# A fill of 1024 columns, with a wait, behind each of 80 indirect DMAs on GpSimd

## The reference, cut to what matters

```python
router_probs = softmax(einsum('bnc,ec->bne', x, router_w))
expert_weights, expert_idx = top_k(router_probs, 2)
expert_weights = expert_weights / (expert_weights.sum(axis=-1, keepdims=True) + 1e-09)
h = gelu(einsum('bnc,efc->bnef', x, expert_w1) + expert_b1)
out_all = einsum('bnef,ecf->bnec', h, expert_w2) + expert_b2
out_k = take_along_axis(out_all, expert_idx[..., None], axis=2)
return (out_k * expert_weights[..., None]).sum(axis=2)
...
x = x + gb * that      # gb: the layer's gate per channel
```

## Time and profile before

| | us |
|---|---|
| median of 3 runs | 1585.96 (1582.42 to 1589.9) |
| span of the profiled execution | 1571.4 |
| median minus that span | 14.6 |
| TensorE busy | 1254.3 (80%) |
| VectorE busy | 938.7 (60%) |
| ScalarE busy | 942.5 (60%) |
| GpSimd busy | 417.8 (27%) |

### The profile page before, as it was taken

How to read it: one execution, slowest core, us unless ns; L and a number is a source line. 1 busy time by engine, 2 the same in 40 slices (tenths; PEclk the granted TensorE clock), 3 DMA queues, 4 the chain that set the end, 5 groups by cost and what they waited for, 6 DMA issues and landing times. The chain is left out here.

```text
span 1571.4 us, 26317 instructions
## 1 busy us (share of the span) xinstructions
PE 1254.3 (80%) x8185; PEld 785.6 (50%) x8186; DVE 938.7 (60%) x2462; ACT 942.5 (60%) x1383; POOL 417.8 (27%) x460
## 2 busy tenths in 40 slices
PE   6996556695878658999999999999999796665660
PEld 4875556695875422333333333333333674564560
DVE  5563343473657747777777777877777575420222
ACT  4563512232325548999999899988999484332330
POOL 5254773414427720000000000000000004545333
PEclk9998768898988879999999999999999898777885
DMA  9600012222223653222222212222220411102222
GB/s 273 202 1 28 28 58 62 67 67 61 69 57 116 201 131 46 37 37 38 35 37 39 38 26 37 37 36 37 38 38 4 135 31 46 51 31 76 72 58 72
DMA packets 114776, 100.34 MB, mean 64 GB/s; under 512 B 10882, under 2 KB 99424, under 8 KB 114656
## 3 DMA queue, kind: packets, MB, share of 16 engines
q1 hardware_dynamic: 101256, 78.64, 20.9%
q0 software_dynamic: 8192, 16.79, 3.7%
q10 hardware_dynamic: 5208, 3.43, 0.9%
HBM read 54.51 MB, written 44.30 MB: 63 GB/s over the span
## 5 line engine op out<-in xcount | busy, mean ns | idle before, releaser
L2392 ACT ACTIVATE probs<-scores_ps 128x1024 f32<-128x1024 f32 x512 | 505.3, 1026 | 61.1 <-PE scores_ps L2419 56.5
L2419 PE MATMUL scores_ps<-q_pack,k_pack 64*128 64x512 f32 x1024 | 247.0, 494 | 47.1 <-ACT probs L2392 27.4
L2436 PE MATMUL pv_ps<-probs,v_pad 128*32 128x512 f32 x2048 | 275.0, 610 | 0.0
L2419 PEld LDWEIGHTS scores_ps<-q_pack,k_pack 64*128 64x128 f32 x1024 | 96.4, 185 | 321.9 <-ACT probs L2392 171.9
L1379 ACT ACTIVATE hidden_experts<-pre_experts 128x512 f32<-128x512 f32 x94 | 59.3, 631 | 184.8 <-DVE pre_experts L1313 79.9
L1401 PE MATMUL up_ps_experts<-x_t_experts,up_weights_now_experts 128*128 128x128 f32 x752 | 114.1, 300 | 68.8 <-issue 30.3
L1401 PEld LDWEIGHTS up_ps_experts<-x_t_experts,up_weights_now_experts 128*128 128x128 f32 x752 | 100.9, 209 | 75.2 <-issue 48.3
L2619 DVE TENSOR_SCALAR_CACHE_REDUCE junk<-sparse_scores,at 128x1024 f32<-128x1024 f32 x96 | 122.8, 1279 | 3.4
L2312 POOL COPY v_pad<-v 128x256 f32<-128x256 f32 (+1 forms) x16 | 6.3, 402 | 434.9 <-PE pv_ps L2436 434.8
L1408 PE MATMUL down_ps_experts<-weights_t,hidden_experts 128*128 x736 | 102.6, 285 | 0.0
L1313 DVE TENSOR_TENSOR pre_experts<-up_ps_experts,weights_t 128x512 f32<-128x512 f32 x94 | 64.5, 686 | 61.0 <-PE up_ps_experts L1401 31.2
(11 more groups left out here) (399 smaller groups left out, 2346.6 us busy)
## 6 DMA issues: line engine op xcount, KB each, us to landing
q_pack<-q_pieces_dram SPq DMA_DIRECT2D x120, 64.0 KB
k_pack<-k_pieces_dram SPq DMA_DIRECT2D x120, 64.0 KB
expert_rows_dram<-zeros SPq DMA_DIRECT2D x1, 6400.0 KB, 21.9
x_rows_experts<-expert_rows_dram SPq DMA_DIRECT2D x25, 256.0 KB
expert_rows_dram<-y_rows_experts SPq DMA_DIRECT2D x46, 128.0 KB
q_pieces_dram<-q_pieces_prep SPq DMA_DIRECT2D x8, 512.0 KB, 3.6
k_pieces_dram<-k_pieces_prep SPq DMA_DIRECT2D x8, 512.0 KB, 3.6
expert_rows_dram<-zeros SPq DMA_DIRECT2D x1, 2560.0 KB, 17.4
```

The costliest lines, as they stand in the source:

```text
L2392: act.activation(probs[:, kt % 2, 2 * pair : 2 * pair + 2, c * 512 : c * 512 + 512], scores_ps[n % 2][:].rearrange("p (h t) -> p h t", h=2 ...
L2419: ins = pe.matmul(scores_ps[n % 2][:, head * 512 : head * 512 + 512], k_pack[group % 2][rows, pair, kt * P : kt * P + P].bitcast(F32R), q_ ...
L2436: ins = pe.matmul(pv_ps[32 * j : 32 * j + 32, c, :], v_pad[:, group % 2, kt, j, :], probs[:, kt % 2, j, c * 512 : c * 512 + 512], start=(k ...
```

## The change

GpSimd gets a buffer `between` of 128 partitions x 1024 columns that nothing reads. A function `apart` fills it with zeros and settles, so that GpSimd's next instruction waits for the fill. `send_rows` and `gather` call `apart` after each indirect DMA, but only where it is given: in the expert loop, that is for the sends of batches 2 and 3 and the gathers of batches 0, 1 and 2. These are 5 chains of 16 DMAs, 80 fills. The stage in front and the stage behind the loop issue theirs as before.

```diff
--- before.py
+++ after.py
@@ -145,7 +145,7 @@
         step.settle()
         step(pool.tensor_tensor(h, h, bc(self.mod0[:, b, MOD0_PARTS.index(SB), :], NT), ALU.add))
 
-    def send_rows(self, g, pool, b, part=0, parts=1):
+    def send_rows(self, g, pool, b, part=0, parts=1, apart=None):
 
         rows = [(k, n) for k in range(2) for n in range(NT)]
         each = len(rows) // parts
@@ -153,6 +153,8 @@
             pool.indirect_dma_start(
                 self.rows, bass.IndirectOffsetOnAxis(ap=g.pick0[:, b, k, n : n + 1], axis=0), self.h[:, b * NT + n, :], None
             ).then_inc(g.rows_sent[b], 16)
+            if apart is not None:
+                apart()
 
     def loads(self, dram):
         return [
@@ -1184,12 +1186,14 @@
         a.clear_sems()
 
 
-def gather(pool, g, picked, b, parts, sem):
+def gather(pool, g, picked, b, parts, sem, apart=None):
 
     for k, n in parts:
         pool.indirect_dma_start(
             picked[k][:, b * NT + n, :], None, g.expert_rows0, bass.IndirectOffsetOnAxis(ap=g.pick0[:, b, k, n : n + 1], axis=0)
         ).then_inc(sem, 16)
+        if apart is not None:
+            apart()
 
 
 def experts0(nc, g, moe, picked):
@@ -1210,6 +1214,7 @@
         pre = a.sb("pre", [P, 2, FC, P])
         hidden = a.sb("hidden", [P, 2, FC, P])
         y_rows = a.sb("y_rows", [P, UNROLL, C])
+        between = a.sb("between", [P, 1024])
         xt_ps = a.ps("xt_ps", [C, UNROLL, P])
         up_ps = [a.ps(f"up_ps{i}", [P, FC, P]) for i in range(2)]
         down_ps = [a.ps(f"down_ps{i}", [P, 512]) for i in range(2)]
@@ -1278,17 +1283,22 @@
             @block.gpsimd
             def _(pool):
                 step = Steps(pool, sum_vec)
+
+                def apart():
+                    step(pool.memset(between[:], 0.0))
+                    step.settle()
+
                 for b in range(B):
                     if b >= SENT_EARLY:
                         moe.scale_and_shift(pool, step, b)
                         step.settle()
-                        moe.send_rows(g, pool, b)
+                        moe.send_rows(g, pool, b, apart=apart)
                     pool.wait_ge(g.rows_sent[b], 16 * 2 * NT)
                     pool.sem_inc(rows_here, moe.tiles)
                 pool.sem_inc(rows_here, max(moe.tiles, 2 * UNROLL))
                 for b in range(B - 1):
                     pool.wait_ge(y_free, b * (2 * AHEAD) + (2 * AHEAD + 1))
-                    gather(pool, g, picked, b, [(k, n) for k in range(2) for n in range(NT)], g.rows_picked)
+                    gather(pool, g, picked, b, [(k, n) for k in range(2) for n in range(NT)], g.rows_picked, apart=apart)
                     if 1 <= b <= EARLY:
                         pool.wait_ge(var_ready, b)
                         g.ln1.invert(pool, b - 1).then_inc(rstd_ready, 1)
```

## The result

| | us |
|---|---|
| changed kernel, median of 4 runs | 1520.68 (1519.96 to 1522.63) |
| kernel before, median of 4 runs | 1587.93 (1582.42 to 1592.06) |
| ratio, 95% interval | 0.9594 (0.9562 to 0.9625) |
| predicted | 1531, range 1515 to 1600 |

The changed kernel is 4.1% faster where the prediction's profile was taken. Both are measured, and the second half of this text is about what differs.

A forecast was written before the change was run, and what follows sets the result against it. TensorE, held up in five chains of back-to-back indirect DMAs, was taken as the bound. Loop end 474.3 to 419 gives 55 us: 1571.4 - 55 = 1516.4, plus 14.6 from span to median, 1531; range 1515 to 1600.

The forecast's parts named there:

- What bounds: Expert loop: TensorE's completions are held up while GpSimd issues indirect DMAs back to back, about 15 us in each of five chains.
- Price of the fill and period: In the five chains: a 1024-column fill takes 0.95 us, and DMA, fill and wait repeat every 2.19 us, at most 2.49.
- TensorE freed: In the chains: pauses free TensorE, with up to 3 us of lateness left per chain; chance 0.70.
- VectorE's wait at step 13: Loop step 13, where VectorE needs GpSimd's weighted sum of batch 0: a new wait of some 15 us, up to 18.
- at the steady pace 309.7: When step 13's transposes come, 14 steps of 7.71 us after the first at 201.78.
- the port's price: VectorE copies beside fills: 0.25 us a tile, some 18 tiles in each of two chains behind step 13; 4 us taken.
- The prediction's own sign: Stated check: if VectorE does not wait at step 13 for GpSimd's weighted sum, TensorE was not freed.
- The loop's end: Last copy of the expert loop: at 413, or 419 with lateness left in two chains, against 474.3 before.
- nothing behind the loop changes: Everything after the expert loop was taken to run as before, so the loop's 55 us gain carries through.
- From span to median: Whole kernel: median put 14.6 us above the profiled span, so 1516.4 became 1531.
- Its own 0.95 us each, pause or not: Rival, in chains: each DMA costs TensorE 0.95 us regardless, fills add port cost; 1586 to 1608, likeliest 1592; chance 0.10.
- Held as long as the chain lasts: Rival, in chains: TensorE stays held throughout the longer chain, losing 26.4 instead of 15 us each; 1643; chance 0.20.

The follow-up runs named there:

- experiment 11: Changed kernel without fills in the last chain, the gather of batch 2, which goes back to back; held: 1535.29 us against 1585.51, ratio 0.9694.
- experiment 12: Changed kernel with chains treated separately: landing waits, back to back, 32 columns, 512 columns, 1024 columns without the wait; held: 1542.24 us against 1585.51.
- free runs: Runs in groups where the unchanged kernel before takes 1373 to 1376 us (median) and its back-to-back chains keep TensorE busy.
- held ones: Runs in groups where the kernel before takes about 1586 us and TensorE loses time in back-to-back chains of indirect DMAs.
- kernel 6: The changed kernel run once more, unchanged, where nothing is held: 1398.73 us, ratio 1.0175 to the kernel before.
- kernel 5: The kernel before run once more, unchanged, with a profile, where nothing is held: 1377.07 us.
- experiments 4: Changed kernel with no fills; GpSimd instead waits after each of the 80 indirect DMAs until it has landed; free: 1441.85 us, ratio 1.0480.
- experiment 10: Kernel of experiment 12 plus a landing wait after each of the 64 sends in layer 1's experts; free: 1464.57 us against 1373.46.
- 2: Changed kernel with fills only behind the 48 gathers, the sends back to back; free: 1381.05 us against 1373.44, ratio 1.0053.

## Why the prediction was right, and where its steps were off

*What bounds.* Right for the place where it was measured. That TensorE loses its time beside indirect DMAs that follow each other closely is shown by experiments 11 and 12, chain by chain. The traces agree over the whole program: in the profile of before all 35 rows whose releaser is "remote" start inside a chain of indirect DMAs or at most 3.5 us behind its end, none in the 787 us between 512.8 and 1299.5, which have no such DMA. In the changed kernel 19 are left, none beside the five chains with fills. What the text did not see is that this is a condition which comes and goes: the profile of one place was taken for the kernel's. The reading that completions came "in a burst only after the last DMA" is too strong as well: its own row at 368.30 started with four DMAs of the chain still to come.

*Price of the fill and period.* 0.95 and 2.19 forecast, 0.97 and 2.21 measured. GpSimd's list came out as worked out: weighted sum of batch 0 done at 328.4 (forecast 327.4).

*TensorE freed.* Yes, and with nothing of the 3 us of lateness a chain that I had left in. The steps ahead of step 13 are 8.8 us in the chains, over the 7.7 to 8.5 that I had named.

*VectorE's wait at step 13.* Forecast at some 15 us, measured 2.3. The step that failed is "at the steady pace 309.7": the port's price was put only behind step 13, at 0.25 us a tile. It was (8.82 - 7.71)/4 = 0.28 us a tile, the right size, but it holds for the 12 steps ahead of step 13 too, and delays VectorE's arrival to 326. As GpSimd's list was the bound there anyhow, one took the place of the other and the sum did not move: that is luck. The prediction's own sign, that TensorE was not freed if VectorE does not wait at step 13, came within 2.3 us of a false alarm. Behind step 13 I had let half of it be hidden, and none was.

*The loop's end.* Forecast 413 without lateness and 419 with it, measured 414.3. The sum used 419, so the loop's gain was 60.4 us and not 55. The term "nothing behind the loop changes" was off by 10 us the other way: behind the last copy the profile has 1106.6 us (1520.9 - 414.3) instead of 1096.6. 4.8 of them are the later start of the next block when GpSimd ends last (8.6 us instead of 3.8). The other 5 have no cause that a run shows; the kernel of experiment 11, whose block begins after 3.8 us, takes 1099.9.

*From span to median.* 1516.4 was forecast for the profiled execution, 1520.9 came, 4.5 more. The median lies 0.2 us under that span and not 14.6 above it. So the 10.3 us between 1531 and 1520.7 are 14.8 too many for the offset, less the 4.5. That 1531 is as near as it is rests in part on these errors against each other.

*The rivals.* "Its own 0.95 us each, pause or not" falls: with landing waits the same 16 DMAs cost nothing. "Held as long as the chain lasts" falls for pauses of 0.8 us and more. With 32 columns, where TensorE is busy 6.20 of 23.50, its size is about right, but not its words: TensorE started products at 284.77 and 289.16, before the last DMA at 295.40. The Trainium skill's sentence that TensorE never waits on anyone ("SBUF — State Buffer", "Who interferes with whom") agrees with the free runs, 19.99 busy of 20.10, and not with the held ones, 7.91 of 19.90. That section is about the ports of SBUF, and no run shows that the held time is spent on a port; where they differ the measurement stands. Its other sentence, on the locked port pair, agrees with the price: the copies of 571 ns take 1177 beside the fills, and in the free case the change costs 23 us, by steps of 8.83 instead of 7.71 and by GpSimd's list. The end of that list in kernel 6, and the same place in kernel 5:

```profile
394.32 1.73 POOL L1670 TENSOR_TENSOR ln_rstd<-ln_var_eps,minus_half 128x8 f32<-128x8 f32 x1
...
404.22 1.62 POOL L1192 DMA_INDIRECT v<-expert_rows_dram,pick  x1 [8.16 <-POOLq L74]
```

```profile
376.16 0.42 DVE L1308 COPY up_weights_now_experts<-weights_t 128x512 f32 x1
...
380.37 1.62 POOL L1190 DMA_INDIRECT v<-expert_rows_dram,pick  x1 [14.49 <-POOLq L74]
```

394.32 + 1.73 is followed by 8.16 us until GpSimd's first instruction in the next block; in kernel 5 the block follows 3.8 us behind the last copy.

*Open.* What the held condition is. It stays for a whole group of runs, and it is not the chip as such. It shows ahead of the loop and in layer 1 too: of the 196.5 us between the two profiled spans of before, 98 lie behind the loop (1571.4 - 474.8 against 1374.9 - 376.6). Nor is it shown what in TensorE is held. "Its results arrive late" is where most of the time shows, but in experiment 12 TensorE also stood still between single matmuls of one product:

```profile
271.93 0.28 PE L1436 MATMUL down_ps_experts<-weights_t,hidden_experts 128*128 x1 [1.84 <-issue]
```
Which core of the chip or which place in memory a program gets was not seen. A kernel with 512 columns throughout costs 0.17% where it is free (0 to 0.35%) and frees TensorE in the one chain in which it was tried held; as a whole it was not run held. If it lies as far below the changed kernel there as in the free case, 1398.7 - 1378.0 = 20.7 us, it would take 1500, an estimate.

## What to carry to other kernels

When an engine is idle in a profile and its releaser has no name, look at what another engine issues at that time, and look at a second profile from another place before the kernel is tuned to it: a gain of 4% here is a loss of 1.75% there. Filling a pause in a chain of indirect DMAs with a write was cheap here while VectorE, whose copies it stretched, had slack; price it by that slack, not by its length. And follow a contention that you price through every stage in which it holds, not only behind the point where the bound changes.

## What the runs showed of the hardware that was not expected

- The same program takes 1374 or 1586 us, in whole groups of runs, on the same chip. In the slower case TensorE's results reach the other engines up to 14 us late beside indirect DMAs 1.25 us apart; every wait released by "remote" lies beside such a chain.
- Pauses of 0.80 us and more between them remove this, those of 0.41 us did not, in the one chain that had them.
- An indirect DMA that is waited for lands 1.5 to 2.8 us after GpSimd has issued it in experiments 4 and 12, mostly 1.5 to 1.9, and up to 4.1 in layer 1 of experiment 10; with 16 such waits TensorE is busy 40.80 of 40.80 us in the held case.
- From GpSimd's last instruction in a block to its first in the next 8.16 us pass where its list ends last (the changed kernel, 2 and 6), while the block begins 3.8 us behind the loop where it does not.
